# A windowed attention block: halved tiles for GpSimd, statistics in pairs, and a later rounding in the MLP

## The chip, the cores and the metric

One core of one Trainium2 chip. The time is the device time of one execution in microseconds, the median of several runs of the same program. The profile is one execution of its own, with a record of each instruction.

## The reference

A Swin-style block over x of 4 x 256 x 256 x 96 in float32: a shift by 4, windows of 8 x 8 tokens, LayerNorm, attention with 3 heads of 32, a residual, LayerNorm, an MLP of 96 to 384 to 96 with exact gelu, a residual, and the shift back.

```python
h = _ln(win, ln1_g, ln1_b)
q = einsum('ntc,chd->nthd', h, wq) + bq        # k and v likewise
attn = softmax(einsum('nqhd,nkhd->nhqk', q, k) / sqrt(32))
win = win + einsum('nqhd,hdc->nqc', einsum('nhqk,nkhd->nqhd', attn, v), wo) + bo
h2 = _ln(win, ln2_g, ln2_b)
win = win + gelu(h2 @ w1 + b1, approximate=False) @ w2 + b2
```

## The kernel before, in words

The tokens are cut into 256 units of 16 windows (1024 tokens: 8 tiles of 128 tokens by 96 channels). Units run in 16 batches of 16. A batch has two stages: sixteen attention steps, then sixteen MLP steps. Between them the unit's tokens stay in SBUF (`stream`). Every engine has its own instruction stream, written out by hand, with loops over the steps, and semaphores alone order them; there is no planner.

**Attention step s** (PE: `attention_step`, L657 on) is a software pipeline over units: PE computes scores of unit s+1, turns the probabilities of unit s (`transpose_probs`, L622), projects q and k of unit s+2 (L576), attends for unit s (`attend`, L637), projects the rest of q and k, turns the normalised tiles of unit s+3 (`transpose1`, L544), projects v of s+2 (L591) and the output of s (L651).

- ACT normalises unit s+3 first (`normalise1`, L742: eight instructions of 128 x 96, one for each tile, since scale and shift are per partition), then copies the turned probabilities (L773), q and k, takes the exponentials (L784), copies the output of attend (L790), the upper half of hT (L760) and v (L778).
- DVE takes maxima (L959), subtracts them (L966), sums (L974) and inverts (L982), forms the lower half of hT (L951), adds attention's output into `stream` (L988) and takes the statistics for the second LayerNorm (L902).
- POOL unites the halves of hT (`unite_hT`, L347), at some steps finishes statistics (`finish1`, `finish2`: nine or ten small dependent instructions, among them the power -0.5 at L379), normalises three early units for the MLP (`normalise2`, L407 and L411) or splits two of them (L417, L423), and last scales the probabilities of unit s+1 (`normalise_probs`, three instructions at L340).

The two halves of float32 operands (upper: rounded to fp32r, lower: the rest) exist since q, k and the first MLP matmul are done in three fp32r steps.

**MLP step j.** PE runs up for unit j's second part, up for unit j+1's first part (L688), then down for unit j (L702). ACT takes the gelus of j's second part, then rounds unit j+2 to its upper half (`copy_h2T_upper`, L839), then takes the gelus of j+1's first part (L830). The rounding waits for a DMA: DVE normalises unit j+3 (L1002, L1009), turns 32 x 32 blocks (L1019), and SP sends them through DRAM and fetches them back (L275, L281). DVE forms the lower half of the first 512 columns (L1026), POOL that of the rest (L429); POOL also adds b2 to `stream` (L436), and DVE adds the result (L988). POOL finishes the statistics of four units per call: `finish2` at j = 1 and 3, `finish1` (for the next batch) at j = 6, 9, 12, and of one unit at 14.

Of the kernel before, what the change touches and what calls it, by code (L numbers as in the profile page):

```python
# [23 lines left out]
ALU = mybir.AluOpType  # L24
# [9 lines left out]
P = 128  # L34
# [6 lines left out]
TILES = TOK // P  # L41
# [14 lines left out]
GELU_AHEAD = FCHUNKS + 1  # L56
LN_GROUP = 4
LN_OPS = 9
LN_CALLS = 12
BLOCK = 32  # L60
CBLOCKS = C // BLOCK
TBLOCKS = P // BLOCK
# [6 lines left out]
def swin_block(nc, x, ln1_g, ln1_b, wq, bq, wk, bk, wv, bv, wo, bo, ln2_g, ln2_b, w1, b1, w2, b2, out):  # L69
# [3 lines left out]
    with ExitStack() as ctx:  # L73
# [8 lines left out]
        def sem(name):  # L82
            return ctx.enter_context(nc.semaphore(name))
# [89 lines left out]
        split_step = sem("split_step")  # L173

        rstd1_ready = sem("rstd1_ready")
        ln1_ready = sem("ln1_ready")
        t1_done = sem("t1_done")
        hT_upper_copied = sem("hT_upper_copied")
        hT_copied = sem("hT_copied")
# [149 lines left out]
        def _(pool):  # L329
# [52 lines left out]
            def finish1(call, u, first, units):  # L382
# [5 lines left out]
                nc.gpsimd.tensor_tensor(shift1[:, first:first + units, :], minus_mean[:, 0:units * TILES].rearrange("p (u t) -> p u t", t=TILES),  # L388
                                        rstd1[:, first:first + units, :], ALU.mult).then_inc(rstd1_ready, units)

            def finish2(call, u, first, units):
                pool.wait_ge(stats2_done, u + units)
                at = LN_OPS * call
                finish_statistics(at, stats2, first, units, 0.5,
                                  mean2[:, first:first + units, :].rearrange("p u t -> p (u t)"), rstd2)
                pool.wait_ge(ln_step, at + LN_OPS)
                pool.sem_inc(rstd2_ready, units)
# [38 lines left out]
                nc.gpsimd.tensor_tensor(now, now, b2_all[:, :].unsqueeze(1).to_broadcast((P, TILES, C)),  # L436
                                        ALU.add).then_inc(b2_added, 1)

            FIRST_CALLS = 21

            def first_attention():

                calls = iter(range(FIRST_CALLS))
                pool.wait_ge(consts_set, 4)
                finish1(next(calls), 0, 0, 1)
                finish1(next(calls), 1, 1, 1)
                unite_hT(0)
                finish1(next(calls), 2, 2, 2)  # L450
                unite_hT(1)
                normalise_probs(0, 0)
                finish1(next(calls), 4, 4, 2)
                for s in range(BATCH):
                    unite_hT(s + 2)
                    if s in (1, 3, 5, 7, 9):
                        finish1(next(calls), s + 5, s + 5, 2)
                    if s == 2:
                        finish2(next(calls), 0, 0, 2)
                    if s in (4, 6, 10):  # L460
                        n = (4, 6, 10).index(s)
                        normalise2(0, n, n)
                    if s == 8:
                        finish2(next(calls), 2, 2, 2)
                    if s == 11:
                        finish1(next(calls), BATCH, 0, 2)
                    if s in (12, 14):
                        n = (s - 12) // 2
                        lower_early(0, n, n, copy_h2T_early(n, n))
                    if s == 13:  # L470
                        finish1(next(calls), BATCH + 2, 2, 1)
                    if s == 15:
                        finish2(next(calls), 4, 4, 2)
                    normalise_probs(s + 1, (s + 1) % 2)
                return next(calls)

            def attention(b):
                batch = b * BATCH
                call = LN_CALLS * (b - 1) + FIRST_CALLS
                for s in range(BATCH):  # L480
                    unite_hT(batch + s + 2)
                    if s == 3:
                        finish2(call, batch, 0, 2)
                    if s == 4:
                        normalise2(b, batch, 0)
                    if s == 5:
                        finish1(call + 1, batch + BATCH, 0, 2)
                    if s == 6:
                        normalise2(b, batch + 1, 1)
                    if s == 7:  # L490
                        finish1(call + 2, batch + BATCH + 2, 2, 1)
                    if s == 8:
                        finish2(call + 3, batch + 2, 2, 2)
                    if s == 9:
                        normalise2(b, batch + 2, 2)
                    if s == 10:
                        finish2(call + 4, batch + 4, 4, 2)
                    if s == 11:
                        lower_early(b, batch, 0, copy_h2T_early(batch, 0))
                    if s == 12:  # L500
                        finish2(call + 5, batch + 6, 6, 2)
                    if s == 13:
                        lower_early(b, batch + 1, 1, copy_h2T_early(batch + 1, 1))
                    normalise_probs(batch + s + 1, (s + 1) % 2)
                return call + 6

            def mlp(b, call, first):
                batch = b * BATCH
                add_b2(batch)
                for j in range(BATCH):  # L510
# [4 lines left out]
                    if first and j == 0:  # L515
                        finish2(call, batch + 6, 6, 2)
                        call = call + 1
                    if j in (1, 3):
                        at = 8 + 2 * (j - 1)
                        finish2(call + j // 2, batch + at, at, LN_GROUP)  # L520
                    if j in (6, 9, 12):
                        at = AHEAD + LN_GROUP * (j // 3 - 2)
                        finish1(call + j // 3, batch + BATCH + at, at, LN_GROUP)
                    if j == 14:
                        finish1(call + 5, batch + 2 * BATCH - 1, BATCH - 1, 1)

            mlp(0, first_attention(), True)
            with batches(mybir.EngineType.Pool, 1) as b:
# [3 lines left out]
        def _(pe):  # L532
# [20 lines left out]
                return isinstance(u, int) and u < 0  # L553

            def transpose1(u, g):
                pe.wait_ge(ln1_ready, 2 * u + g + 1)
                if g == 0:
                    need(shift_done, HEADS * (u - 2) + 1)
                else:
# [177 lines left out]
        def _(act):  # L737
# [1 line left out]
            def absent(u):  # L739
                return isinstance(u, int) and u < 0  # L740

            def normalise1(u, index, g):  # L742

                if g == 0:
                    wait_apart(act, rstd1_ready, u + 1)
                    if not (isinstance(u, int) and u == 0):
                        wait_apart(act, t1_done, 2 * u)
                slot = u % SLOTS if isinstance(u, int) else u & (SLOTS - 1)
                for t in range(g * (TILES // 2), (g + 1) * (TILES // 2)):
                    last = nc.scalar.activation(normed1[:, t, :], stream[:, slot, t * C:(t + 1) * C], ACT.Identity,  # L750
                                                bias=shift1[:, index, t:t + 1], scale=rstd1[:, index, t:t + 1])
                last.then_inc(ln1_ready, 1)

            def copy_hT_upper(u, g):

# [39 lines left out]
            def attention_step(u, half, index):  # L795


                back, middle, front = u, u + 1, u + 2
                for g in range(2):
                    normalise1(u + 3, index, g)  # L800
                if not absent(back):
                    for h in range(HEADS):
                        copy_probsT(back, h)
# [59 lines left out]
            with batches(mybir.EngineType.Activation) as b:  # L863
# [4 lines left out]
                        attention_step(batch + 2 * r + half, half, (2 * r + half + AHEAD) & (BATCH - 1))  # L868
                nc.scalar.preload_act_table_set("gelu_and_others")
                gelus(batch, 0, 0)  # L870
                with act.Fori(0, BATCH // 2 - 1) as k:
                    for odd in (0, 1):
                        j = 2 * k + odd
                        gelus(batch + j, odd, 1)
                        copy_h2T_upper(batch + j + 2, odd)
                        gelus(batch + j + 1, 1 - odd, 0)
                gelus(batch + BATCH - 2, 0, 1)
                gelus(batch + BATCH - 1, 1, 0)
                gelus(batch + BATCH - 1, 1, 1)
# [265 lines left out]
```

## Time and profile before

| | |
|---|---|
| median of 3 runs | 5110.54 us (5109.84 to 5123.42) |
| the profiled execution | 5120.26 us, span 5118.4 us |
| PE busy | 4931.8 us (96%) |
| PE weight load busy | 4154.1 us (81%) |
| DVE busy | 4072.6 us (80%) |
| ACT busy | 3873.0 us (76%) |
| POOL busy | 3623.5 us (71%) |
| HBM traffic | 80 GB/s over the span |

A share is an average over both stages, which have different limits. Matmuls are pipelined and their ends modelled, so a busy PE may still be held up between groups by fractions of a microsecond.

### The profile page before, as it was taken

What the parts mean: (1) busy time and instruction counts of PE and PEld (TensorE: products, weight loads), DVE (VectorE), ACT (ScalarE), POOL (GpSimd) and SP (SyncE); (2) the same over time, 40 slices, a digit from 0 to 9 for tenths busy, and PEclk for the clock granted to TensorE, in tenths of its full rate; (3) what the DMA queues carried; (4) which work ended last, traced back from release to release, by engine and by line L of the source; (5) the groups of instructions that cost most, each with busy time, mean ns of one, the idle gap of its engine ahead of it and who ended that gap; (6) DMA issues with size and microseconds to landing.
All of it is one profiled execution on the core that took longest, in us unless ns stands there. A gap on an engine that the chain in (4) does not pass through costs nothing.

```text
span 5118.4 us, 275139 instructions
## 1 busy us (share of the span) xinstructions
PE 4931.8 (96%) x103124; PEld 4154.1 (81%) x103124; DVE 4072.6 (80%) x9254; ACT 3873.0 (76%) x8206; POOL 3623.5 (71%) x3589
## 2 busy tenths in 40 slices
PE   7999999999999999999999999999999999999999
PEld 6888888888888888888888888887888888888887
DVE  8969778697786977869788796887968879698786
ACT  7859688595886958769587695976949769496794
POOL 6868667686676866767767677676776767777676
PEclk9999999999999999999999999999999999999999
DMA  3141331313213132131322314223042230422304
GB/s 109 34 119 54 94 94 42 116 48 102 86 48 116 42 111 77 56 113 37 117 74 62 112 33 123 68 68 109 26 123 68 74 108 24 124 65 77 108 26 122
DMA packets 222028, 410.68 MB, mean 80 GB/s; under 512 B 29225, under 2 KB 131850, under 8 KB 221898
## 3 DMA queue, kind: packets, MB, share of 16 engines
q1 hardware_dynamic: 220336, 409.06, 27.0%
q14 instruction: 122, 1.00, 0.1%
q10 hardware_dynamic: 1562, 0.50, 0.0%
q8 instruction: 8, 0.13, 0.0%
HBM read 208.11 MB, written 201.33 MB: 80 GB/s over the span
## 4 chain that ended last, share of the span: by engine, by line
PE 55%; DVE 16%; DMA 9%; issue 8%; SPq 7%; ACT 2%; DVEq 2%; POOL 1%; ACTq 0%; POOLq 0%
PE psum L576 12%; PE psum L702 6%; PE psum L591 6%; PE psum L622 6%; PE psum L651 5%; PE psum L608 5%; PE psum L688 5%; PE psum L637 5%; DMA oT<-turned_rows 5%; DMA turned_rows<-normed 4%; SPq L269 4%; PE psum L544 4%; DVE normed L1002 3%; SPq L275 2%; DVE normed L1009 2%
## 5 line engine op out<-in xcount | busy, mean ns | idle before, releaser
L340 POOL TENSOR_TENSOR probs<-probs,prob_inv 128x512 f32<-128x512 f32 x771 | 783.1, 1043 | 839.6 <-DVE prob_inv L982 836.2
L988 DVE TENSOR_TENSOR stream<-stream,psum 128x384 f32 (+1 forms) x1024 | 547.1, 549 | 298.5 <-PE psum L702 225.0
L750 ACT ACTIVATE normed<-stream,shift,rstd 128x96 f32 (+1 forms) x2072 | 770.5, 461 | 17.8 <-issue 16.1
L902 DVE BATCH_NORM_STATS2 stats<-stream 128x6 f32 (+2 forms) x4224 | 721.3, 243 | 58.0 <-DVE stream L988 29.4
L379 POOL TENSOR_TENSOR rstd<-variance,minus_half 128x8 f32<-128x8 f32 (+2 forms) x201 | 745.0, 3707 | 15.7
L347 POOL TENSOR_TENSOR hT<-hT_upper,hT_lower 96x1024 f32<-96x1024 f32 x258 | 614.2, 2380 | 11.8 <-DVE hT_lower L951 6.8
L702 PEld LDWEIGHTS psum<-w_w,gelu_odd 128*64 128x64 f32 x12288 | 512.4, 137 | 59.4 <-issue 59.4
L974 DVE TENSOR_REDUCE prob_sum<-probs 128x8 f32<-128x512 f32 x771 | 492.5, 678 | 84.2 <-ACT probs L784 84.1
L966 DVE TENSOR_TENSOR probs<-psum,row_max 128x512 f32<-128x512 f32 x771 | 533.2, 692 | 26.6
L830 ACT ACTIVATE gelu_odd<-psum 128x512 f32<-128x512 f32 x768 | 418.7, 593 | 174.8 <-PE psum L688 156.5
L702 PE MATMUL psum<-w_w,gelu_odd 128*64 128x96 f32 x12288 | 536.4, 247 | 12.2 <-ACT gelu_odd L830 12.2
L702 PEld LDWEIGHTS psum<-w_w,gelu_even 128*64 128x64 f32 x12288 | 511.1, 137 | 45.4 <-issue 45.4
L959 DVE TENSOR_REDUCE row_max<-psum 128x8 f32<-128x512 f32 x771 | 522.3, 677 | 26.0 <-PE psum L608 19.5
L702 PE MATMUL psum<-w_w,gelu_even 128*64 128x96 f32 x12288 | 535.2, 247 | 0.0
L839 ACT ACTIVATE h2T_odd_upper<-oT 96x512 fp32r<-96x512 f32 x224 | 129.0, 623 | 536.2 <-DMA oT<-turned_rows 536.2
L436 POOL TENSOR_TENSOR stream<-stream,b_all 128x768 f32 (+1 forms) x256 | 490.9, 1920 | 15.0 <-POOL rstd L379 14.0
L784 ACT ACTIVATE probs<-probs 128x512 f32<-128x512 f32 x771 | 463.7, 629 | 28.7 <-DVE probs L966 25.1
L576 PE MATMUL psum<-hT_upper,qk_split_upper 128*96 128x512 f32 x1032 | 455.1, 441 | 1.9 <-DVE hT_lower L951 1.9
L830 ACT ACTIVATE gelu_even<-psum 128x512 f32<-128x512 f32 x768 | 408.6, 592 | 23.6 <-PE psum L688 8.5
L773 ACT ACTIVATE probsT<-psum 128x512 f32<-128x512 f32 x768 | 396.0, 587 | 38.0 <-PE psum L622 38.0
L637 PEld LDWEIGHTS psum<-probsT,v 64*32 64x32 f32 x24576 | 277.5, 105 | 169.0 <-issue 168.3
L576 PE MATMUL psum<-hT_lower,qk_split_upper 128*96 128x512 f32 x1032 | 408.9, 396 | 0.0
(94 smaller groups left out, 11327.9 us busy)
## 6 DMA issues: line engine op xcount, KB each, us to landing
turned_rows<-normed SPq DMA_DIRECT2D x624, 128.0 KB
stream<-in_x SPq DMA_DIRECT2D x272, 192.0 KB
out<-stream SPq DMA_DIRECT2D x256, 192.0 KB
stream<-in_x SPq DMA_DIRECT2D x272, 180.0 KB
out<-stream SPq DMA_DIRECT2D x256, 180.0 KB
probsT<-turned_rows SPq DMA_DIRECT2D x112, 384.0 KB, 3.2
oT<-turned_rows SPq DMA_DIRECT2D x112, 384.0 KB, 3.2
turned_rows<-gelu_odd SPq DMA_DIRECT2D x144, 128.0 KB
```

The source lines that it names most:

```text
L340: nc.gpsimd.tensor_tensor(block_h, block_h, inv, ALU.mult).then_inc(probs_ready, 1)
L347: nc.gpsimd.tensor_tensor(hT[0:C, :], hT_split[0][0:C, :], hT_split[1][0:C, :], ALU.add)\
L379: nc.gpsimd.tensor_tensor(flat(rstd), variance[:, 0:n], minus_half[:, 0:n], ALU.pow)\
L576: last = nc.tensor.matmul(psum[0:C, QK_BANKS[n], :], qk_split[w][:, which, :], hT_split[h][:, group * SHARES:(group + 1) * SHARES], start= ...
L637: last = nc.tensor.matmul(psum[KD * h:KD * (h + 1), PV_BANKS[parity], at:at + WT], v[keys, buffer, quad, w, KD * h:KD * (h + 1)], probsT[k ...
L702: last = nc.tensor.matmul(psum[WT * side:WT * (side + 1), DOWN_BANKS[part], t * C:(t + 1) * C], gelu[parity][:, j, c * P + WT * side:c * P ...
L750: last = nc.scalar.activation(normed1[:, t, :], stream[:, slot, t * C:(t + 1) * C], ACT.Identity, bias=shift1[:, index, t:t + 1], scale=rs ...
L830: nc.scalar.activation(in_rows[:, 2 * part:2 * part + 2, :, :], psum[:, UP_BANKS[part][j], :].rearrange("p (b t i) -> p b t i", b=2, i=BLOCK),
L902: last = nc.vector.bn_stats(stats[:, index, c, :], stream[:, slot, c * C:(c + 1) * C])
L959: nc.vector.tensor_reduce(row_max[:, h, :], psum[:, S_BANKS[h], :].rearrange("p (t k) -> p t k", k=WT), AXIS.X, ALU.max).then_inc(max_step, 1)
L966: nc.vector.tensor_tensor(probs[:, buffer, h, :, :], psum[:, S_BANKS[h], :].rearrange("p (t k) -> p t k", k=WT), row_max[:, h, :].unsqueez ...
L988: nc.vector.tensor_tensor(part, part, psum[:, banks[g], 0:GROUP], ALU.add).then_inc(added, 1)
```

## The change

Three edits.

1. In attention POOL normalises tiles 0 to 3 of each unit, with two instructions of 128 x 384 (times rstd, plus shift, both broadcast along the channels), after `unite_hT` of the step and ahead of any statistics call; ACT normalises tiles 4 to 7 only. `ln1_ready` becomes two semaphores, and PE waits for each half by itself.
2. In the MLP every statistics call covers two units: `finish2` at j = 1, 2, 3, 5, `finish1` at j = 4, 6, 8, 10, 12, 13, 14 (the last of one unit).
3. In the MLP ACT's rounding of unit j+2 stands behind the gelus of unit j+1's first part. Since those gelus write where the early units' turned blocks lie, ACT waits once per MLP for the DMAs that read them.

```diff
+            def normalise1_first(u):
+                index = u & (BATCH - 1)
+                tiles = slice(0, TILES // 2)
+                def per_tile(stat):
+                    return stat[:, index, tiles].unsqueeze(2).to_broadcast((P, TILES // 2, C))
+                wait_apart(pool, rstd1_ready, u + 1)
+                if not (isinstance(u, int) and u == 0):
+                    wait_apart(pool, t1_done, 2 * u - 1)
+                nc.gpsimd.tensor_tensor(normed1[:, tiles, :],
+                                        stream[:, u & (SLOTS - 1), 0:GROUP].rearrange("p (t c) -> p t c", c=C),
+                                        per_tile(rstd1), ALU.mult).then_inc(scale1_step, 1)
+                pool.wait_ge(scale1_step, u + 1)
+                nc.gpsimd.tensor_tensor(normed1[:, tiles, :], normed1[:, tiles, :], per_tile(shift1), ALU.add)\
+                    .then_inc(ln1_ready[0], 1)
...
                 for s in range(BATCH):
                     unite_hT(batch + s + 2)
+                    normalise1_first(batch + s + 3)
...
+            SECOND = (1, 2, 3, 5)
+            FIRST = (4, 6, 8, 10, 12, 13, 14)
+            ORDER = sorted(SECOND + FIRST)
...
-                    if j in (1, 3):
-                        at = 8 + 2 * (j - 1)
-                        finish2(call + j // 2, batch + at, at, LN_GROUP)
-                    if j in (6, 9, 12):
-                        at = AHEAD + LN_GROUP * (j // 3 - 2)
-                        finish1(call + j // 3, batch + BATCH + at, at, LN_GROUP)
-                    if j == 14:
-                        finish1(call + 5, batch + 2 * BATCH - 1, BATCH - 1, 1)
+                    if j in SECOND:
+                        at = 8 + 2 * SECOND.index(j)
+                        finish2(call + ORDER.index(j), batch + at, at, 2)
+                    if j in FIRST:
+                        at = AHEAD + 2 * FIRST.index(j)
+                        units = min(2, BATCH - at)
+                        finish1(call + ORDER.index(j), batch + BATCH + at, at, units)
...
-                pe.wait_ge(ln1_ready, 2 * u + g + 1)
+                pe.wait_ge(ln1_ready[g], u + 1)
...
-                for t in range(g * (TILES // 2), (g + 1) * (TILES // 2)):
+                for t in range(TILES // 2, TILES):
...
+                wait_apart(act, h2_left, 16 * CBLOCKS * (batch + AHEAD))
                 with act.Fori(0, BATCH // 2 - 1) as k:
                     for odd in (0, 1):
                         j = 2 * k + odd
                         gelus(batch + j, odd, 1)
+                        gelus(batch + j + 1, 1 - odd, 0)
                         copy_h2T_upper(batch + j + 2, odd)
-                        gelus(batch + j + 1, 1 - odd, 0)
```

## Rows read from the trace of the kernel before

**Rows 1.** The page, chain of work that ended last, shares of the span by engine.

```profile
PE 55%; DVE 16%; DMA 9%; issue 8%; SPq 7%; ACT 2%; DVEq 2%; POOL 1%; ACTq 0%; POOLq 0%
```

**Rows 2.** Windows, batch 6: stretch, length, each engine's busy us (instructions), clock, DMA.

```profile
1951.60:2117.10 165.50, 160.26 (x4321) 133.18 (x4320) 150.26 (x357) 160.68 (x360) 122.15 (x126) 1.00 0.18 51
...
1984.60:1996.10 11.50, 10.98 (x296) 9.11 (x302) 11.18 (x32) 10.72 (x26) 9.56 (x10) 1.00 0.39 117
...
2007.00:2018.30 11.30, 10.73 (x292) 8.85 (x293) 11.02 (x25) 10.70 (x26) 10.05 (x13) 1.00 0.18 53
...
2106.30:2117.10 10.80, 10.54 (x288) 8.85 (x288) 10.10 (x24) 10.68 (x25) 5.38 (x4) 1.00 0.00 0
```

**Rows 3.** Timeline (start, us long, engine, line, what) of ACT and PE before the attend matmuls.

```profile
2106.34 1.18 PE L637 MATMUL psum<-probsT,v 64*32 64x64 f32 x96 [0.36 <-ACT probsT L773]
...
2115.20 1.54 ACT L773 ACTIVATE probsT<-psum 128x512 f32<-128x512 f32 x3
...
2115.29 0.48 PE L576 MATMUL psum<-hT_upper,qk_split_upper 128*96 128x512 f32 x1
...
2117.13 1.18 PE L637 MATMUL psum<-probsT,v 64*32 64x64 f32 x96 [0.21 <-issue]
...
2265.84 1.57 ACT L773 ACTIVATE probsT<-psum 128x512 f32<-128x512 f32 x3 [2.50 <-PE psum L622]
...
2266.43 0.47 PE L576 MATMUL psum<-hT_upper,qk_split_upper 128*96 128x512 f32 x1
...
2267.99 1.19 PE L637 MATMUL psum<-probsT,v 64*32 64x64 f32 x96
```

**Rows 4.** Timeline, ACT: the eight normalise instructions of a unit.

```profile
2112.33 2.97 ACT L750 ACTIVATE normed<-stream,shift,rstd 128x96 f32 x8
```

**Rows 5.** Timeline, POOL in attention: a pair call, probs, unite, and idle time.

```profile
2006.46 0.24 POOL L360 TENSOR_TENSOR mean_gap<-stats 128x16 f32<-128x16 f32 x1
...
2012.44 3.05 POOL L340 TENSOR_TENSOR probs<-probs,prob_inv 128x512 f32<-128x512 f32 x3 [0.77 <-DVE prob_inv L982]
...
2102.77 2.39 POOL L347 TENSOR_TENSOR hT<-hT_upper,hT_lower 96x1024 f32<-96x1024 f32 x1
...
2110.99 3.05 POOL L340 TENSOR_TENSOR probs<-probs,prob_inv 128x512 f32<-128x512 f32 x3 [5.83 <-DVE prob_inv L982]
```

**Rows 6.** Groups by line: busy us, mean ns | idle before.

```profile
L340 POOL TENSOR_TENSOR probs<-probs,prob_inv 128x512 f32<-128x512 f32 x771 | 783.1, 1043 | 839.6 <-DVE prob_inv L982 836.2 <-PE psum L591 3.5
...
L407 POOL TENSOR_TENSOR normed<-stream,mean 128x768 f32<-128x768 f32 x48 | 70.6, 1472 | 0.4 <-DVE gelu_odd L1019 0.4
```

**Rows 7.** Waits, whole span: total us, times, longest.

```profile
PE psum L688 <- DVE h2T_even_lower L1026: 22.2, 13, 3.0
...
PE psum L688 <- ACT gelu_even L830: 18.1, 24, 1.5
```

**Rows 8.** Timeline, MLP: two stalls of PE, and ACT around the second.

```profile
2205.89 0.47 PE L688 MATMUL psum<-h2T_even_upper,w_split_upper 128*128 128x512 f32 x1 [1.64 <-DVE h2T_even_lower L1026]
...
2212.70 1.16 ACT L839 ACTIVATE h2T_odd_upper<-oT 96x512 fp32r<-96x512 f32 x2 [7.81 <-DMA oT<-turned_rows]
...
2213.76 2.99 ACT L830 ACTIVATE gelu_even<-psum 128x512 f32<-128x512 f32 x6
...
2215.44 0.47 PE L688 MATMUL psum<-h2T_odd_upper,w_split_upper 128*128 128x512 f32 x1 [0.89 <-ACT gelu_even L830]
```

**Rows 9.** Timeline, MLP: DVE beside POOL's b2 addition and beside its power.

```profile
2197.55 3.62 DVE L1009 TENSOR_TENSOR normed<-normed,rstd 128x768 f32<-128x768 f32 x1
...
2198.53 1.82 POOL L436 TENSOR_TENSOR stream<-stream,b_all 128x768 f32 x1
...
2215.27 1.00 POOL L360 TENSOR_TENSOR mean_gap<-stats 128x32 f32<-128x32 f32 x1
...
2218.93 5.44 POOL L379 TENSOR_TENSOR rstd<-variance,minus_half 128x32 f32<-128x32 f32 x1
...
2223.86 0.96 DVE L1009 TENSOR_TENSOR normed<-normed,rstd 128x768 f32<-128x768 f32 x1
```

More of the change, by code:

```diff
@@ L58 @@
 LN_OPS = 9
-LN_CALLS = 12
+LN_CALLS = 17
 BLOCK = 32
@@ L175, in swin_block @@
         rstd1_ready = sem("rstd1_ready")
-        ln1_ready = sem("ln1_ready")
+        scale1_step = sem("scale1_step")
+        ln1_ready = [sem("ln1_ready_first"), sem("ln1_ready_second")]
         t1_done = sem("t1_done")
@@ L437, in add_b2 @@
                                         ALU.add).then_inc(b2_added, 1)
-            FIRST_CALLS = 21
+            FIRST_CALLS = 26
             def first_attention():
@@ L447, in first_attention @@
                 finish1(next(calls), 0, 0, 1)
+                normalise1_first(0)
                 finish1(next(calls), 1, 1, 1)
                 unite_hT(0)
+                normalise1_first(1)
                 finish1(next(calls), 2, 2, 2)
+                normalise1_first(2)
                 unite_hT(1)
@@ L455, in first_attention @@
                     unite_hT(s + 2)
+                    normalise1_first(s + 3)
                     if s in (1, 3, 5, 7, 9):
@@ L740, in absent, with normalise1_second @@
                 return isinstance(u, int) and u < 0
[L742 to L747, printed above, removed]
+            def normalise1_second(u, index):
+                wait_apart(act, rstd1_ready, u + 1)
+                if not (isinstance(u, int) and u == 0):
+                    wait_apart(act, t1_done, 2 * u)
                 slot = u % SLOTS if isinstance(u, int) else u & (SLOTS - 1)
-                for t in range(g * (TILES // 2), (g + 1) * (TILES // 2)):
+                for t in range(TILES // 2, TILES):
                     last = nc.scalar.activation(normed1[:, t, :], stream[:, slot, t * C:(t + 1) * C], ACT.Identity,
                                                 bias=shift1[:, index, t:t + 1], scale=rstd1[:, index, t:t + 1])
-                last.then_inc(ln1_ready, 1)
+                last.then_inc(ln1_ready[1], 1)
             def copy_hT_upper(u, g):
@@ L798, in attention_step @@
                 back, middle, front = u, u + 1, u + 2
-                for g in range(2):
-                    normalise1(u + 3, index, g)
+                normalise1_second(u + 3, index)
                 if not absent(back):
```

## The prediction

> **What bounds the kernel now.** I read the chain of waits first: the chain that ended last is mostly TensorE (55%), with VectorE (16%), DMA and issue behind it [rows 1]. TensorE looks like the limit, at one clock throughout (granted 1.00, the 2.4 GHz level [rows 2]), so only the places where it is held up can be won. The question is who holds it, and that differs by stage, so I cut one batch (batch 6) into its sixteen attention steps and its MLP. The reader should see in [rows 2] that ScalarE is busy 160.68 of the 165.50 us between the batch's first and last attend, 10.7 us in every step, whatever the step's length (10.8, 11.3 or 11.5). No other column is that flat: GpSimd goes from 5.38 us in a plain step to 10.05 in one with a statistics call. An engine whose busy time never falls below the step is one that sets it.
>
> The timeline shows how. The attend matmuls (L637) wait for the last copy of the turned probabilities (L773). ACT ends these copies at 2115.20 + 1.54 = 2116.74 and attend starts at 2117.13, 1.84 us after the first projection matmul of the step (2115.29). In the first step of the next batch ACT had been waiting for TensorE (2.50 us idle) and the same distance is 2267.99 - 2266.43 = 1.56 [rows 3]. So a plain step of 10.8 us holds 0.3 us of waiting for ACT and TensorE's own step is 10.5. In every second step the distance is some 0.3 us longer, with ACT named as the releaser, 0.36 us idle before 2106.34 [rows 3].
>
> In the MLP ScalarE is far from busy; there TensorE waits 22.2 us in 13 places for VectorE's lower half of h2T and 18.1 us in 24 places for gelu [rows 7].
>
> **Pool norms tiles 0 to 3.** ACT loses four of eight normalise instructions per unit, half of 2.97 us, 1.5 us per step [rows 4]. A step's ACT work falls to 10.7 - 1.5 = 9.2 us, and the copies that attend waits for need only trail the transposes, as in the floor step. ACT's bound is gone; its gain depends on who is next.
>
> GpSimd gains two tensor_tensor of 128x384. No row shows that size. The same form takes 1043 ns at 512 and 1472 at 768 elements [rows 6], a slope of 1.68 ns, so 828 ns each; from both sides, half of the 768 (736 ns) and the whole of the 512 (1043). I take 828, it follows from both rows. The second waits for the first by a semaphore (under 0.1 us). So 1.73 us per step (1.5 to 2.15).
>
> Its plain step is then 5.38 + 1.73 = 7.1 us of 10.5 and hides. The others must be counted. Its extras in a batch (the pair calls at s = 3, 5, 8, 10, 12, the single call at 7, the three normalise2, the two early lowers) are all in s = 3 to 13. They are 122.15 - 15 x 5.38 = 41.5 us busy [rows 2]; a call also has gaps at its semaphores: the one from 2006.46 to the probs at 2012.44, less 0.77 idle, takes 5.2 us [rows 5], and about 0.5 of that is gaps, so 3 us for six calls. Those eleven steps need 11 x 7.1 + 44.5 = 122.7 us on GpSimd. Today they take 2106.3 - 1984.6 = 121.7 us [rows 2]; TensorE's floor is 11 x 10.5 = 115.5. So ACT's bound is replaced by GpSimd's, at nearly the same height. What GpSimd can be late without harm is small: the probs start on inv_ready (idle 5.83 us before it in a plain step, 0.77 in one with a call [rows 5]), and heads 0 to 2 end 1.0, 2.0 and 3.05 us later, against transposes some 1.2 us into the next step; that leaves about 0.9 us, once. So the eleven steps take 122.7 - 0.9 = 121.8: nothing won. The four others (s = 0, 1, 2, 14) go from 165.5 - 121.7 = 43.8 to 4 x 10.5 = 42.0, and I give 0.2 back to s = 2, whose VectorE has a second set of statistics (11.18 us busy in the step after [rows 2]). A batch wins 1.5; sixteen win 24. The first batch has further GpSimd calls in steps 1 to 9 and could lose 2 to 5 us; with it, **attention: -22 us**.
>
> What is queued behind the two new waits on GpSimd: for rstd1_ready its own earlier work, for the first transposes of the unit before (t1_done), long past. Behind the new instructions stand the statistics call and the next unit's probs, which TensorE waits for, and that is counted above. TensorE's own transposes of tiles 0 to 3 now wait for GpSimd: probs start + 3.0 + 2.4 + 1.7 = 7.1 us, against a need at 3.1 + 0.4 + 1.6 + 1.1 + 1.5 = 7.7 us after it when GpSimd is late, so 0.6 us is left. VectorE's operands in attention come from PSUM or are single, so I see nothing for the new instructions to collide with.
>
> **ACT's rounding behind gelu.** The rounding of unit j+2 waits for its DMA (7.81 us idle before 2212.70), and the gelus of j+1 queue behind it until 2213.76, though their matmuls were done; TensorE stands 0.89 us for them at 2215.44 [rows 8]. Put behind, the gelus no longer wait. The rounding is not later where the DMA is the last to arrive, as it is in nearly all steps of this MLP; where the DMA is early it is later by three gelus, about 1.5 us, with over 2 us to spare before the next up. So the 18.1 us [rows 7] go, and VectorE's lower half is not late in their place: it ends within 1.4 us of the rounding's start. The added wait for h2_left is for DMAs of attention steps 5 to 11 and costs nothing. **-18 us** (bounds: -20, 0).
>
> **Statistics in pairs.** Five calls of four units become ten of two, each with ten instructions. A call of four runs from 2215.27 to 2218.93 + 5.44 = 2224.37 and a last small one, 9.3 us; the pair call takes 5.2 [rows 5, 9]. So 5 x (10.4 - 9.3) = 5 us more GpSimd work per MLP (11 if VectorE blocks each small instruction), on an engine that is idle in 29% of the span. But steps 1 to 6 now all hold a call: 5.2 + 1.8 for b2 + 1.3 for the lower = 8.3 to 9.5 us against a step of 8.4, so GpSimd may trail by up to 6 us at step 6. Its lower half is for the second part of up, about 7 us later: just covered. What is won: after a long call, b2, lower and b2 came in a row, and VectorE's two-input instruction stood still under them, 3.62 us for one that takes 0.96 [rows 9]; the lower after it came late, and TensorE waited 1.64 [rows 8]. With shorter calls a third of the 22.2 us goes by my estimate, between all of it and 20 us more, since the b2 additions now fall on VectorE's instructions in more steps. **-8 us**.
>
> The Trainium skill (SBUF, "Who interferes with whom") says that a VectorE instruction with two SBUF inputs and a GpSimd one that reads SBUF exclude each other for the whole instruction. For b2 the trace agrees: VectorE's instruction from 2197.55 ends at 2201.17, 0.8 us after the addition of 2198.53 to 2200.35. For the power it does not: at 2223.86 VectorE needs its usual 0.96 us inside a power of 5.44 [rows 9]. By the page, cutting the power from 5.4 to 2.9 would free VectorE too, and all 22 us might go, 14 us more than my sum: 5048, inside my own range, and I give it 0.05 of the forecast's chance since the row speaks against it.
>
> Sum, against the profiled execution (5118.4 of span, 5120.3 in all): -22 - 18 - 8 = -48, so 5072. The median of the runs shown is 10 us lower, 5110.5, and the forecast goes from there: **5062 us**.
>
> **Rivals.** (a) GpSimd's lateness costs more than it does in the sum. Steps are not averaged: a step with a call (12.3) is not repaid by a light one (10.5), because there is one probs buffer ahead only. Then s = 3 to 13 cost 5 x 12.2 + 10.8 + 5 x 10.5 = 124.3 instead of 121.8, +40 us over sixteen batches, and if in the MLP six calls in a row hold VectorE 1.2 us more per step than its slack, +2 per batch, +32. Result 5062 + 72 = 5134, slower than before. It decides as soon as the calls' lag is not carried over. For it: 0.77 us idle in the call steps today. Against: light and heavy steps alternate and the slack of 0.9 us is used each time. (b) ACT was the whole limit and GpSimd's lag is absorbed: all fifteen steps at 10.6, 165.5 to 159, -100 us for attention, 4985. Against it is the count of 122.7. Half of it, with instructions nearer 736 ns, gives some 5025. (c) The attention exchange is exactly level and the MLP's stalls only change their names: within 0.3%, 5095 to 5126.
>
> **Chances.** Forecast (5035 to 5095) 0.46; (b) whole or half 0.18; (c) 0.16; (a) 0.20. The range 5010 to 5125 leaves out the far half of (a) and of (b). About 0.3% is what can be told from no change. Faster by more than that: 0.46 + 0.18 = 0.64; within: 0.16; slower: 0.20.
>
> **What would show it.** ACT's busy time in an attention step near 9.2 us; steps 0, 1, 14 at 10.5 with attend 1.56 us after the first projection; GpSimd without idle time in steps 3 to 13, and TensorE's transposes of probs waiting for L340 there; no wait of L688 for gelu; power instructions of 128x32 gone. Wrong would be: call steps still at 11.3 with GpSimd idle (another limit), new instructions over 1 us each, or MLP steps longer than 8.4 us in a row.

## The result, and the profile after

| | before | changed |
|---|---|---|
| median | 5118.62 us (5 runs) | 5137.05 us (5 runs, 5133.89 to 5141.25) |
| span of the profiled execution | 5118.4 us | 5138.1 us |
| ratio | 1 | 1.0041 (95% interval 1.0029 to 1.0054) |

(With two more runs the median of before is 5118.62 instead of the 5110.54 shown ahead; the ratio is to it.) The change made the kernel slower by 0.4%, where 0.9% faster was forecast. Its place can be read stage by stage. The starts of the attend and the down matmuls in the timeline cut each trace into the same stretches; summed over the sixteen batches, from the first to the last attend and from the first to the last down:

| us | before | changed | difference |
|---|---|---|---|
| attention, batches 1 to 15, each | 165.54 | 164.53 | -1.01, in all -15 |
| attention, first batch | 168.5 | 174.4 | +6 |
| MLP, sixteen batches | 2065.5 | 2093.1 | **+27.6** |
| start, to the first attend | 49.8 | 50.9 | +1 |

So attention won 8 us with the start counted in, and the MLP lost nearly 28. The page's busy times and the chain of the changed kernel (before: TensorE 55% of the chain [rows 1]):

```profile
PE 4929.3 (96%) x103124; PEld 4145.0 (81%) x103124; DVE 4183.5 (81%) x9254; ACT 3677.9 (72%) x7170; POOL 4242.9 (83%) x4875
...
POOL 33%; issue 18%; PE 16%; DVE 10%; SPq 10%; DMA 9%; POOLq 1%; DVEq 1%; ACT 1%; ACTq 0%
```

TensorE's busy time did not move; GpSimd's rose by 620 us and it leads the chain. The windows of batch 6, as in [rows 2] (stretch, length, busy us and instructions of PE, PEld, DVE, ACT, POOL, clock, DMA):

```profile
1966.20:2130.70 164.50, 159.77 (x4321) 132.82 (x4320) 150.03 (x357) 145.18 (x301) 144.48 (x155) 1.00 0.18 52
...
1997.80:2009.30 11.50, 10.75 (x289) 8.96 (x288) 11.18 (x32) 9.56 (x21) 10.92 (x16) 1.00 0.41 111
...
2020.20:2032.00 11.80, 10.96 (x289) 8.85 (x288) 11.48 (x26) 9.75 (x21) 11.25 (x16) 1.00 0.23 68
...
2119.90:2130.70 10.80, 10.53 (x289) 8.87 (x288) 10.41 (x24) 9.59 (x21) 7.35 (x8) 1.00 0.00 0
```

ScalarE is down from 10.7 to 9.7 us per step (145.18 / 15), where the prediction had 9.2, GpSimd up from 122.15 to 144.48 over the fifteen steps, and the last step is still a 10.8. The two new instructions of GpSimd, and its probs in two call steps, where before it had idle time ahead [rows 5]:

```profile
L403 POOL TENSOR_TENSOR normed<-stream,rstd 128x384 f32<-128x384 f32 x259 | 214.0, 826 | 0.5 <-POOL shift L389 0.5
...
L407 POOL TENSOR_TENSOR normed<-normed,shift 128x384 f32<-128x384 f32 x259 | 214.8, 829 | 20.3
...
2014.72 3.04 POOL L341 TENSOR_TENSOR probs<-probs,prob_inv 128x512 f32<-128x512 f32 x3 [0.73 <-DVE prob_inv L1008]
...
2026.89 3.04 POOL L341 TENSOR_TENSOR probs<-probs,prob_inv 128x512 f32<-128x512 f32 x3
```

The price was right (826 and 829 ns against 828 forecast), and at 2026.89 there is no idle time any more in front of the probs. TensorE now waits for them, in 118 places, and in the MLP for VectorE's odd lower half, 37.2 us against 2.4 before, and still for gelu (before: [rows 7]):

```profile
PE psum L649 <- POOL probs L341: 38.2, 118, 0.4
...
PE psum L715 <- DVE h2T_odd_lower L1052: 37.2, 43, 1.4
...
PE psum L715 <- ACT gelu_even L855: 16.5, 16, 1.3
...
PE psum L715 <- DVE h2T_even_lower L1052: 16.4, 12, 1.8
```

### The profile page after: what moved, and what is told of

Read it like the earlier page. It is cut to its first block, busy times and chain, and to the rows that moved or that the text cites. A ratio compares the mean times of both kernels' runs of the same rounds, so it can differ in the third digit from the quotient of the medians.

```text
span 5138.1 us, 275192 instructions
## 1 busy us (share of the span) xinstructions
PE 4929.3 (96%) x103124; PEld 4145.0 (81%) x103124; DVE 4183.5 (81%) x9254; ACT 3677.9 (72%) x7170; POOL 4242.9 (83%) x4875
## 4 chain that ended last, share of the span: by engine, by line
POOL 33%; issue 18%; PE 16%; DVE 10%; SPq 10%; DMA 9%; POOLq 1%; DVEq 1%; ACT 1%; ACTq 0%
POOL hT L348 8%; POOL probs L341 7%; POOL rstd L380 7%; DMA oT<-turned_rows 6%; SPq L270 6%; DVE normed L1028 4%; PE psum L603 4%; DMA turned_rows<-normed 3%; DVE normed L1035 3%; SPq L276 3%; POOL normed L403 3%; PE psum L715 3%; DVE normed L1045 2%; POOL normed L407 2%; PE psum L729 2%
## 5 line engine op out<-in xcount | busy, mean ns | idle before, releaser
L380 POOL TENSOR_TENSOR rstd<-variance,minus_half 128x16 f32<-128x16 f32 (+1 forms) x281 | 779.8, 2775 | 22.0
L855 ACT ACTIVATE gelu_odd<-psum 128x512 f32<-128x512 f32 x768 | 455.6, 597 | 226.2 <-PE psum L715 179.4
L799 ACT ACTIVATE probsT<-psum 128x512 f32<-128x512 f32 x768 | 416.2, 599 | 275.8 <-PE psum L649 275.7
L855 ACT ACTIVATE gelu_even<-psum 128x512 f32<-128x512 f32 x768 | 441.3, 593 | 110.4 <-PE psum L715 71.4
L455 POOL TENSOR_TENSOR stream<-stream,b_all 128x768 f32 (+1 forms) x256 | 480.0, 1878 | 18.7 <-POOL rstd L380 17.5
L649 PE MATMUL psum<-ident,probs 128*128 128x128 f32 x3072 | 416.6, 279 | 38.4 <-POOL probs L341 38.2
L776 ACT ACTIVATE normed<-stream,shift,rstd 128x96 f32 (+1 forms) x1036 | 399.4, 464 | 21.4 <-issue 19.2
```

The costliest lines, as they stand in the source:

```text
L380: nc.gpsimd.tensor_tensor(flat(rstd), variance[:, 0:n], minus_half[:, 0:n], ALU.pow)\
L855: nc.scalar.activation(in_rows[:, 2 * part:2 * part + 2, :, :], psum[:, UP_BANKS[part][j], :].rearrange("p (b t i) -> p b t i", b=2, i=BLOCK),
```

## The hold-up of VectorE in the MLP

Before, these were the three instructions of VectorE in the MLP that read two inputs from SBUF (subtract, scale, lower; busy us, mean ns):

```profile
L1002 DVE TENSOR_TENSOR normed<-stream,mean 128x768 f32 (+1 forms) x208 | 305.8, 1470 | 48.2 <-issue 38.8
...
L1009 DVE TENSOR_TENSOR normed<-normed,rstd 128x768 f32<-128x768 f32 x208 | 255.3, 1227 | 24.2
...
L1026 DVE TENSOR_TENSOR h2T_even_lower<-probsT,h2T_even_upper 96x512 fp32r<-96x512 f32 x112 | 101.5, 906 | 65.2 <-ACT h2T_even_upper L839 65.0
...
L1026 DVE TENSOR_TENSOR h2T_odd_lower<-oT,h2T_odd_upper 96x512 fp32r<-96x512 f32 x112 | 86.5, 773 | 301.3 <-ACT h2T_odd_upper L839 301.3
```

and in the changed kernel:

```profile
L1028 DVE TENSOR_TENSOR normed<-stream,mean 128x768 f32 (+1 forms) x208 | 337.5, 1622 | 33.8 <-issue 27.9 <-POOLq L416 2.3
...
L1035 DVE TENSOR_TENSOR normed<-normed,rstd 128x768 f32<-128x768 f32 x208 | 316.4, 1521 | 24.1
...
L1052 DVE TENSOR_TENSOR h2T_even_lower<-probsT,h2T_even_upper 96x512 fp32r<-96x512 f32 x112 | 130.4, 1164 | 33.3 <-ACT h2T_even_upper L864 32.6
...
L1052 DVE TENSOR_TENSOR h2T_odd_lower<-oT,h2T_odd_upper 96x512 fp32r<-96x512 f32 x112 | 85.9, 767 | 289.2 <-ACT h2T_odd_upper L864 289.1
```

Undisturbed they take 0.95, 0.96 and 0.69 us. What they take beyond that I call blocked time: 208 x (1470 - 950) ns and so on, 198 us before and 322 us after (both with 1 to 4 us of two set-up copies). Nearly all of it lies under GpSimd's long instructions. Each held instruction, put down to the GpSimd instruction that it overlaps longest, gives 183 of the 198 us to b2 additions before; after, 269 us to b2 additions and 41 us to GpSimd's own lower halves. The subtracts and scales held by a b2 addition end 0.81 to 0.82 us after it in nearly every case, which is most of their own 0.95 us. A single case, changed kernel, last but one batch; GpSimd's b2, lower, b2 in a row, VectorE under them, and what became of it:

```profile
4743.96 1.85 POOL L455 TENSOR_TENSOR stream<-stream,b_all 128x768 f32 x1
...
4745.76 2.00 POOL L448 TENSOR_TENSOR h2T_odd_lower<-oT,h2T_odd_upper 96x512 fp32r<-96x512 f32 x1
...
4747.72 1.82 POOL L455 TENSOR_TENSOR stream<-stream,b_all 128x768 f32 x1
...
4744.11 2.51 DVE L1028 TENSOR_TENSOR normed<-stream,mean 128x768 f32 x1 [0.17 <-issue]
...
4746.74 3.61 DVE L1035 TENSOR_TENSOR normed<-normed,rstd 128x768 f32<-128x768 f32 x1
...
4750.60 0.98 DVE L1045 STREAM_TRANSPOSE normed<-normed 128x768 f32<-128x768 f32 x1 [0.25 <-DVE normed L1035]
...
4762.09 1.15 ACT L864 ACTIVATE h2T_odd_upper<-oT 96x512 fp32r<-96x512 f32 x2 [5.50 <-DMA oT<-turned_rows]
...
4763.68 0.47 PE L715 MATMUL psum<-h2T_odd_upper,w_split_upper 128*128 128x512 f32 x1 [1.35 <-DVE h2T_odd_lower L1052]
```

The scale starts under GpSimd's lower half, does not get in between that and the b2 addition of 4747.72 to 4749.54, takes 3.61 us and ends at 4750.35, 0.8 us after the addition. The block transpose is late by it, so the DMA lands late and the rounding starts at 4762.09; TensorE stands 1.35 us before 4763.68.

Why is it not absorbed? The median distance from a turn (the block transpose) to the rounding of the same unit is 11.4 to 11.5 us in every kernel here but those of experiments 6 and 7 (10.7 to 13.9 in the kernel before, half of them within 0.2 us of 11.4). One round of the loop, in the kernel before:

```profile
2146.69 0.98 DVE L1019 STREAM_TRANSPOSE normed<-normed 128x768 f32<-128x768 f32 x1 [0.24 <-DVE normed L1009]
...
2158.13 1.15 ACT L839 ACTIVATE h2T_odd_upper<-oT 96x512 fp32r<-96x512 f32 x2 [3.99 <-DMA oT<-turned_rows]
...
2158.79 0.69 DVE L1026 TENSOR_TENSOR h2T_odd_lower<-oT,h2T_odd_upper 96x512 fp32r<-96x512 f32 x1 [2.16 <-ACT h2T_odd_upper L839]
...
2159.40 1.01 DVE L988 TENSOR_TENSOR stream<-stream,psum 128x384 f32 x2
...
2160.99 1.30 DVE L1002 TENSOR_TENSOR normed<-stream,mean 128x768 f32 x1 [0.58 <-issue]
...
2162.41 0.96 DVE L1009 TENSOR_TENSOR normed<-normed,rstd 128x768 f32<-128x768 f32 x1
...
2163.61 0.98 DVE L1019 STREAM_TRANSPOSE normed<-normed 128x768 f32<-128x768 f32 x1 [0.24 <-DVE normed L1009]
```

Turn at 2146.69, rounding at 2158.13, lower, two additions, subtract and scale of the unit two later, turn at 2163.61: 16.9 us for two steps. TensorE needs 2 x 8.41 = 16.8. The subtract in this round is itself held for 0.35 us; without any hold-up a round comes to some 16.6 us, and rounds under 16.0 us are rare in the kernel before (the shortest is 15.4). Each unit is turned behind the lower half of the unit two before it, so of a microsecond that VectorE stands still in this loop little is made up in the next round; the rest eats the lead that the MLP starts with and then shows as a stall, which is why the first steps of an MLP are 8.4 us and the stalls come after them.

## Experiments

All ratios are to the kernel before, on the same chip (its median there was 5123 to 5127 us).

**1. The rounding alone.**

```diff
                         gelus(batch + j, odd, 1)
+                        gelus(batch + j + 1, 1 - odd, 0)
                         copy_h2T_upper(batch + j + 2, odd)
-                        gelus(batch + j + 1, 1 - odd, 0)
```

> The kernel before with ACT's rounding behind gelu alone. Theory A (the statistics calls in pairs cost the time in the MLP): this edit by itself does not lose; TensorE's waits for gelu in L688-type matmuls (18.1 us before) shrink, MLP sum from first to last down of each batch 2065 us before becomes 2045 to 2065, total -5 to -20 us. Rival B (the later rounding is what lengthened the MLP): MLP sum 2080 or more, total +15 us or more. Attention the same in both.

0.9993 (0.9984 to 1.0003), MLP 2070.5 us. It does not lose, and it does not win either: the 2045 to 2065 us expected of theory A were missed, and so were the 2080 of B. The wait for gelu is gone (0.2 us), and the same time stands under the lower half, 48.6 us against 24.6:

```profile
PE psum L688 <- DVE h2T_even_lower L1027: 27.6, 14, 2.9
...
PE psum L688 <- DVE h2T_odd_lower L1027: 21.0, 19, 2.4
```

The wait only changed its name: both hung on the same late DMA.

**2. The pairs alone.**

```diff
-                    if j in (1, 3):
-                        at = 8 + 2 * (j - 1)
-                        finish2(call + j // 2, batch + at, at, LN_GROUP)
+                    if j in SECOND:
+                        at = 8 + 2 * SECOND.index(j)
+                        finish2(call + ORDER.index(j), batch + at, at, 2)
...
```

> The kernel before with the statistics of the MLP in pairs alone. Theory A: six calls in a row, 9.3 to 9.6 us of POOL work per step of 8.4, so POOL trails and its b2 addition and lower half fall on VectorE's two-input instructions: MLP sum +25 to +40 us over the 2065 of before, total +25 to +40 us, waits of the up matmuls for VectorE's lower half from 25 us to over 50. Rival B: MLP sum within 8 us of before.

1.0044 (1.0028 to 1.0060), MLP 2090.5 us, +25. So this edit is the loss. The loss starts early in the MLP: the second and third round of the loop in batch 6 took 16.2 and 16.9 us before and take 17.5 and 18.9 here. The waits were expected at the lower half; with the rounding ahead of gelu they stand at gelu, 74 times:

```profile
PE psum L691 <- ACT gelu_even L833: 63.5, 74, 2.3
```

The blocked time is 236 us against 198, and the scale has the whole of the rise (1227 ns before):

```profile
L1005 DVE TENSOR_TENSOR normed<-stream,mean 128x768 f32 (+1 forms) x208 | 308.6, 1484 | 36.7 <-issue 30.5
...
L1012 DVE TENSOR_TENSOR normed<-normed,rstd 128x768 f32<-128x768 f32 x208 | 293.8, 1413 | 24.2
```

By the same overlap count the b2 additions hold VectorE for as long as before (187 us against 183), though more of it in the scale (66 against 50); what is new are 42 us under GpSimd's lower halves, against less than 1 us. They come later when GpSimd trails, and meet the next subtract or scale. Which of the two shifts costs the 25 us is not separated here.

**3. GpSimd's half of the norm alone** (calls of four, rounding ahead of gelu).

> The kernel before with POOL norming tiles 0 to 3 alone. Both theories: attention of batches 1 to 15 shorter by 1.0 us each (-15), the first batch longer by 6, MLP as before: total -8 us (-3 to -14). A third theory C (the attention edit also hurts the MLP, since POOL enters it late) would show the MLP sum up by 10 us or more here.

0.9971 (0.9963 to 0.9980), MLP 2069.2. Attention of batches 1 to 15 164.5 us each, the first batch +4.5. As expected, theory C is out.

**4. The changed kernel with calls of four.**

```diff
-LN_CALLS = 17
+LN_CALLS = 12
...
-                    if j in SECOND:
+                    if j in (1, 3):
...
```

> The changed kernel with calls of four units in the MLP again, so the Pool norm and the later rounding together. Theory A: the sum of the two edits that do not hurt, 5118 - 8 - 12 = about 5098 on the scale on which before is 5118; MLP sum 2065 or less. Rival B: over 5118, since the later rounding is still in it.

0.9977 (0.9967 to 0.9987), MLP 2070.4: the other two edits together are faster than before. The rounding adds nothing to the 0.9971 of the norm alone; the 20 us that I gave the two in the expectation were 12, and the MLP is 5 us over the 2065 expected. The three edits are nearly additive: the spans of the profiled executions moved by +3.9 (rounding), +22.9 (pairs) and -10.1 us (norm), in all +16.7, and by +19.7 with all three.

**5. Pairs, with a power in place of the b2 addition.** Blocked or late? This one takes the long addition away and leaves GpSimd its load: the power reads 9 elements per partition instead of 768. The kernel leaves b2 out.

```diff
-                nc.gpsimd.tensor_tensor(now, now, b2_all[:, :].unsqueeze(1).to_broadcast((P, TILES, C)),
-                                        ALU.add).then_inc(b2_added, 1)
+                wait_apart(pool, b2_added, u)
+                nc.gpsimd.tensor_tensor(spare_out[:, 0:9], spare_in[:, 0:9], minus_half[:, 0:9],
+                                        ALU.pow).then_inc(b2_added, 1)
```

> The pairs alone, but POOL's b2 addition (1.84 us, reads SBUF for both inputs) is left out and a power of 9 elements stands in its place (some 1.8 us of POOL by the slope of 158 ns an element between the powers of 8 and 16, and it did not hold up VectorE in any of 87 cases before). b2 is left out of the result. Theory P (VectorE's two-input instructions stand behind POOL's two-input ones, and the loop turn, DMA, rounding, lower, add, turn has no room for it): the blocked time of subtract, scale and lower falls from 236 us to under 120, MLP sum from 2090 to 2040 or less. Theory L (POOL trails with six calls in a row, and its lateness holds the MLP): POOL as busy as before, MLP sum stays at 2080 to 2095.

0.9870 (0.9853 to 0.9887), MLP 2004 us, where sixteen MLPs without a stall (fourteen steps of 8.41 and one of 7.2 us) are 1999. GpSimd has about the same load: 1974 ns for each power against 1909 for each addition of experiment 2 (1.82 to 1.85 us undisturbed), 3799 us busy in all against 3824. No other engine waits for it in the MLP, as none did in experiment 2:

```profile
L438 POOL TENSOR_TENSOR spare_out<-spare_in,minus_half 128x9 f32<-128x9 f32 x256 | 505.4, 1974 | 32.1 <-POOL rstd L381 28.6 <-POOL spare_out L438 2.9
...
L1008 DVE TENSOR_TENSOR normed<-stream,mean 128x768 f32 (+1 forms) x208 | 225.7, 1085 | 53.0 <-issue 43.3
...
L1015 DVE TENSOR_TENSOR normed<-normed,rstd 128x768 f32<-128x768 f32 x208 | 234.7, 1129 | 24.2
```

Blocked time 65 us, 46 of them under GpSimd's lower halves, about as many as in experiment 2. So without the additions the pairs cost nothing, and theory L falls: a loaded GpSimd does not hold the MLP by itself. It still trails here, but by less: the power that replaces the b2 addition starts 5.2 us after the down matmuls of step 6 on average, the addition 7.7 us in experiment 2. Experiment 12 tests the additions at an almost equal lag.

**6 and 7. The fetch ahead of the store on SP,** in the kernel before and with the pairs.

```diff
-                        store(batch_row + 2 * q + n // 2, n % 2)
                         fetch_late(batch + 4 * q + n + 4, n)
+                        store(batch_row + 2 * q + n // 2, n % 2)
```

> The kernel before, with SP's fetch of a turned unit ahead of the store that stood before it. Theory P: the fetch comes earlier than 8.0 us after the turn in steps whose store has six DMAs, the loop has more room than 0.3 us in two steps, and VectorE's blocked time no longer reaches TensorE: MLP sum 2065 becomes 2010 to 2040, total -25 to -55 us. Theory L: nothing changes in the MLP (fetch is not what waits). If the fetch is bound by its own DMA's landing in every step: copy stays 11.4 us after the turn and the time too.

> The pairs alone, with the same exchange on SP. Theory P: the 25 us that pairs cost go as well, MLP sum within 15 us of that of the exchange without pairs. Theory L: pairs still cost 25 us over the exchange alone.

1.0642 (1.0628 to 1.0655) and 1.0645 (1.0632 to 1.0659), against every expectation; the MLP went from 2065 to 2395 us. SP's queue in the first of them:

```profile
2283.42 1.79 SPq L275 DMA_DIRECT2D turned_rows<-normed  x3
...
2289.99 0.34 SPq L281 DMA_DIRECT2D probsT<-turned_rows  x1
...
2300.88 4.16 SPq L269 DMA_DIRECT2D out<-stream  x6
...
2305.58 1.79 SPq L275 DMA_DIRECT2D turned_rows<-normed  x3
```

The send ends at 2285.21 and the fetch goes only at 2289.99, 4.8 us later, though no store stands between: by the program it waits for the send's landing, and the six stores used to fit into that wait. Now they come after the fetch and the next send stands behind them (from 2300.88 to 2305.04). In batch 6, from the third such unit on, the send left 2.3 to 5.4 us after the turn instead of 1.1, a round of the loop took 21.5 us instead of 17.0 (medians), and TensorE's MLP steps grew with it. TensorE, which stood still more, had a granted clock of 0.95 in the MLP of batch 6 where it had 1.00 before; what part of the time is due to that is not separated. It was a bad way to make room, but a measure of the loop: it has next to none. Both kernels have the same time, so the pairs make no difference behind such a delay, and the two runs tell nothing between P and L.

**8. GpSimd norms tiles 0 and 1 only** (calls of four, rounding late).

```diff
+POOL_TILES = 2
...
-                tiles = slice(0, TILES // 2)
+                tiles = slice(0, POOL_TILES)
...
                 pe.wait_ge(ln1_ready[g], u + 1)
+                if g == 0:
+                    wait_apart(pe, ln1_middle, u + 1)
...
-                for t in range(TILES // 2, TILES):
+                for t in range(POOL_TILES, TILES):
```

> POOL norms tiles 0 and 1 only, ACT 2 to 7, with the later rounding and calls of four (against it: the same with tiles 0 to 3, 5113). My count: two instructions of 128x192 at 507 ns, 1.08 us on POOL instead of 1.73, so steps 3 to 13 need 11 x 6.46 + 44.5 = 115.6 us, TensorE's own 115.5; ACT 9.95 us a step. Attention of a batch falls from 164.5 to 159 to 161, total 5113 - 16 x 4.5 = 5040 (5025 to 5065). If instead the chain through the probabilities and not POOL's load is what sets the call steps, they stay at 11.5 to 12.0 and the total within 15 us of 5113.

0.9885 (0.9870 to 0.9899), 5063 us. Attention 161.6 us a batch instead of 164.5; the prices were 509 and 507 ns:

```profile
L405 POOL TENSOR_TENSOR normed<-stream,rstd 128x192 f32<-128x192 f32 x259 | 131.9, 509 | 0.5 <-POOL shift L391 0.5
...
L780 ACT ACTIVATE normed<-stream,shift,rstd 128x96 f32 (+1 forms) x1554 | 585.3, 464 | 21.3 <-issue 18.0 <-POOL shift L391 2.7
```

It supports the count of attention from the other side, in part: with 0.65 us less per step the call steps 8, 10 and 12, which took 11.5 to 12.0 us, take 10.6 to 10.9. But steps 3 to 13 take 119.0 us where 115.6 was expected, and attention misses its 159 to 161. Steps 3 and 4 stay at 11.5 and 10.9 us, as in every kernel here, while GpSimd stands idle ahead of the probs (0.7 and 1.5 us): it is not what holds them. In step 3 VectorE has 11.18 us of work [rows 2].

**9. One tile.** The same with `POOL_TILES = 1`.

> POOL norms tile 0 only, ACT 1 to 7, else as in the run with two tiles. ACT 10.3 us a step, POOL 0.7 us more than before a step: both under TensorE's 10.5 in nearly all steps, but attend's distance from the first projection comes back by some 0.1 to 0.3 us. Attention 160.5 to 163 us a batch against 161.6 with two tiles, total within 20 us of it.

0.9892 (0.9876 to 0.9907); attention 162.1. One and two tiles can't be told apart by the ratio; both are far better than four.

**10. The b2 addition beside the transpose.** From experiment 8, with one wait:

```diff
-                        add_b2(batch + j + 1)
+                        add_b2(batch + j + 1, batch + min(j + 3, BATCH - 1))
...
-                wait_apart(pool, ln2_ready, u + 1)
+                wait_apart(pool, ln2_ready, (u if scaled is None else scaled) + 1)
```

> The best so far (POOL norms tiles 0 and 1, calls of four, later rounding; 0.9885 of before, MLP sum 2065 us), and POOL's b2 addition of a step waits until VectorE has scaled unit j+3, so that it runs beside the block transpose and the statistics, which have one SBUF input. Theory P: VectorE's blocked time falls from 245 us to 100 to 180, MLP sum 2065 to 2020 to 2050, ratio to before 0.980 to 0.986. If the waits that hold VectorE come only in the steps right after a statistics call, where POOL is late anyway, the new wait changes nothing: 0.987 to 0.990.

**0.9772 (0.9758 to 0.9785), 5009 us**: the fastest, 2.3% under before, better than the range given. MLP 2014.3 us, blocked time 110, and the lower half is hardly waited for:

```profile
L1034 DVE TENSOR_TENSOR normed<-stream,mean 128x768 f32 (+1 forms) x208 | 252.6, 1214 | 40.3 <-issue 33.2
...
L1041 DVE TENSOR_TENSOR normed<-normed,rstd 128x768 f32<-128x768 f32 x208 | 251.4, 1209 | 24.2
...
PE psum L719 <- DVE h2T_odd_lower L1058: 2.8, 6, 0.7
```

**11. The same with the rounding ahead of gelu.**

> The same with ACT's rounding ahead of the gelus again, as before. Theory P: the place of the rounding matters little (it was 0.9993 alone); with VectorE less blocked the wait for gelu is what is left, so this one is slower than the one with the later rounding by 0 to 20 us.

0.9800 (0.9787 to 0.9814), MLP 2034. So the later rounding is worth 0.28% once the loop has room, and was worth nothing before.

**12. The wait in the changed kernel itself.**

> The changed kernel as it is (pairs, four tiles), with the b2 addition waiting until VectorE has scaled unit j+3. If the loss of the pairs is that POOL is loaded beyond the step in j = 1 to 6, so that b2 arrives where it arrives whatever it waits for: blocked time of VectorE 180 to 260 us (322 before this edit), MLP sum 2050 to 2080, ratio 0.996 to 1.001. If it is only where b2 falls, as in the calls of four with the wait: blocked time near 110 us, MLP sum 2010 to 2025, ratio 0.988 to 0.991.

0.9905 (0.9888 to 0.9921), MLP 2028.6 us, blocked time 197: blocked as in the first case, time nearly as in the second. The wait alone takes back 64 of the MLP's 94 us over the floor of 1999. GpSimd still trails: on average the b2 addition of step 6 starts 7.0 us after the down matmuls instead of 8.1, and that of step 7 7.5 instead of 8.4 (in steps 2 and 3 they are 2 us earlier than without the wait). So the gain is in the main where the additions fall. With six calls in a row they now hit the scale most:

```profile
L1028 DVE TENSOR_TENSOR normed<-stream,mean 128x768 f32 (+1 forms) x208 | 250.3, 1203 | 34.5 <-issue 27.6
...
L1035 DVE TENSOR_TENSOR normed<-normed,rstd 128x768 f32<-128x768 f32 x208 | 285.9, 1375 | 24.2
```

In order of blocked time (us) the MLP (us) runs: 65: 2004, 110: 2014, 126: 2034, 197: 2029, 198: 2066, 217: 2069, 236: 2091, 238: 2071, 241: 2066, 245: 2065, 251: 2070, 322: 2093. The two go together only roughly, since where in the loop the blocking falls counts too: the pairs alone have as much as the rounding alone and lose 20 us more, and the kernel of experiment 12 (197) has as much as the kernel before (198) and is 37 us faster. The subtract separates better (experiments 6 and 7 aside): it is held for 108 to 140 us where the MLP takes 2065 us or more, and for 28 to 55 us in experiments 5, 10, 11 and 12. That is read off the runs; no run changes the subtract alone.

## Why the prediction was wrong, step by step

- **What bounds attention.** Right in the main. ACT held attend, and with its share gone attend comes 1.56 us after the first projection (mean 1.56 over all steps; before 1.91). ACT's busy time fell by 1.0 us a step, not 1.5, and attend's distance is at its floor all the same.
- **GpSimd as the next bound, steps 3 to 13: 121.8 us.** Right in steps 5 to 13, where GpSimd has 0.2 to 0.6 us idle per step, and 1997.9 to 2119.9 is 122.0. That the sum fits so well is in part luck: steps 3 and 4 have another limit (experiment 8). The four others came to 42.5 instead of 42.2. **Attention: -22 us** was 8 us won: 15 in batches 1 to 15 (24 x 15/16 = 22.5 forecast), less 6 in the first batch and 1 at its start. Half of the miss is 0.5 us per batch, most of it step 14, which is still 10.8; the other half is the first batch, which lost 6 us where the sum has 0.5 (1.5 won, 2 lost).
- **Rounding: -18 us.** This step failed. It was worked out that "VectorE's lower half is not late in their place". It was: experiment 1 shows 18.1 us of gelu waits gone and 24 us of lower waits come. I had checked that the rounding is not later, not whether what stands behind gelu has the same cause. The term was 0 us, not -18 (0.9993, MLP +5).
- **Pairs: -8 us.** This is the step that turned the sign; it measured +25 us (experiment 2), just beyond its own worst bound of +20. The text named the mechanism ("the b2 additions now fall on VectorE's instructions in more steps") and then took the small gain, because it looked for cover in GpSimd's deadline of 7 us, which was indeed kept. It did not look at VectorE's loop through SP and the DMA, which had nothing left. In the runs the additions hold VectorE, and the loop hands that on to TensorE (experiments 5, 10 and 12). A third fewer stalls was a guess without a row.
- **Rival (a)** gave 5134 and the sign. Its part in attention is refuted (lag is carried over, steps alternate 11.8, 10.6, 10.5, 11.6, and GpSimd is hardly idle in the light ones); its part in the MLP, six calls in a row that hold VectorE, is what happened. That its number is so near is luck: it has 40 us more than the forecast in attention and 32 in the MLP, where 14 and 54 were measured, and the median of before lay 8 us higher. I had given it 0.20.
- **The signs.** The powers of 128x32 are gone and GpSimd has no idle time to speak of in steps 5 to 13, as named. ACT's 9.2 us, step 14 at 10.5 and the end of the waits for gelu (16.5 us are left) did not come, and MLP steps over 8.4 us, named as a sign of being wrong, did.
- **The rule of the Trainium skill** (SBUF, "Who interferes with whom"): the traces agree for GpSimd's additions and subtractions, in the strong form of whole instructions (ends 0.81 to 0.82 us after them). They do not agree for the power, and experiment 5 rests on that. The row that the prediction gave for it was weak: VectorE's instruction from 2223.86 overlaps the power, which ends at 2224.37, for 0.5 us only; whole cases are counted in the last section. The rival worked out from the rule (5048) did not come: shorter powers freed nothing, since powers had blocked nothing.

## What to carry to other kernels

Follow the loop in which a late instruction comes back to itself, through queues and DMAs, and compare its length with the bound engine's step; an engine that is 80% busy can have next to no slack. A wait that disappears from a list has gained nothing until its neighbour in the list has been asked for the same cause. Two engines that shut each other out were better separated in time, with one wait, than by cutting the work into smaller pieces: here the smaller pieces met more often.

## What was not expected of the hardware

- A power on GpSimd of 8 to 32 elements per partition (1.65 to 5.44 us) does not hold up a VectorE instruction with two SBUF inputs; an addition of 1.84 us does, to its end. Of such instructions that lie whole inside a power in the kernel before, 65 lower halves took 686 to 691 ns and 23 subtracts 947 to 959 ns, their usual times. In experiment 5 the 192 cases include 56 scales (957 to 964 ns), and the longest delay is some 40 ns.
- A power of 9 elements takes 1974 ns where the line between 8 (1651) and 16 (2913) gives 1809.
- From the end of the send's issue to the fetch that waits for its landing it is 4.8 to 5.0 us (medians) with no store between. From turn to rounding the median is 11.4 us whether two or six stores are issued in it (94 and 96 cases in the kernel before).
